# Second layer's matmuls split into 16-bit parts, attention's sequence loop written out, maxima issued ahead of exponentials

## The chip, the cores and the metric

One core of a Trainium2 chip runs the whole program. The metric is device time in microseconds (us), the median over several runs. The engines are PE (TensorE, matmuls; PEld is its weight load), DVE (VectorE), ACT (ScalarE), POOL (GpSimd) and SP (SyncE, which issues the DMAs). Each engine runs its own instructions in order and waits on semaphores for the others.

## The reference

The input x is 8 sequences of 512 tokens with 128 features, float32. Four layers follow each other, each as `x = x + layernorm(layer(layernorm(x)))`:

1. A GRU with 256 hidden units over the 512 tokens of each sequence, and a projection back to 128 features (`w_out`). The recurrence is sequential in the token.
2. A feed-forward layer with 8 experts: logits from `gate_W`, the best expert per token, `relu(x wi^T + wi_b + lora_i(x))` of width 512 with a rank-4 correction of that expert, and `wo` back to 128.
3. Attention with 16 heads of width 16, a causal mask, a position term, a smeared key, a silu gate and an output projection.
4. A SwiGLU feed-forward layer of width 384 with integer weights.

## The kernel before

The code is one program in four blocks, each with a hand-written order for every engine.

**Set-up** transposes and splits the GRU's weights into a high and a low fp16 part (W1, W2 for the state, V1, V2 for the input), and writes the normalised, transposed first 128 tokens of all sequences into Y1 and Y2 (fp16 high and low part). Their layout is `[feature, token, sequence]`, so the tokens of one sequence lie 16 bytes apart.

**GRU block.** 512 steps; a step treats all 8 sequences at once. Gate sums lie in PSUM: pR, pZ, pN. PE's `steps` does 36 products of a 128x128 fp16 weight tile with 8 columns of the state (L653): first those with the state's high part G1, then those with its low part G2, and then `inject` puts the next steps' biases (L661, a 3-row bf16 matmul) and input products (L666) into PSUM: two bias and six input matmuls in steps with k = 0 and 1, four bias ones at k = 2, six input ones at k = 3, where k is the step modulo U = 4. ACT's `steps` takes tanh of pR (tr, L805), of pZ (tz, L807) and of v_ (n_, L809). DVE's `steps` makes u_, v_, zg, zn, the new state's high part (L896), the full state HR (L901) and the low part (L903). After every four steps SP copies HR to HS, which keeps all the states.

A function `schedule` lays other work between the steps: every step is a slot, and sixteen slots make a unit. In the first 128 steps (8 rounds q of 16 slots) `prepare` normalises and transposes the remaining tokens of sequence q (ACT L849 writes Y1, DVE L1004 writes Y2, 384 tokens each) and transposes all later weights. In the remaining 384 steps each unit holds one tile of 128 tokens: `early(u, s)` does the GRU's output projection, its layer norm and the gate logits of tile u, and `late(u - 1, s)` does the expert layer of the tile before. 24 of the 32 tiles run beside steps; the last 8 units have no steps left to run beside, and then a last `late` follows. The matmuls of `early` and `late` have float32 operands: L714 and L716 (`woutT`), L725 (transpose of XF), L729 (`gaT`, gate and lora_A), L732 (transpose of the masked ML), L739 (`wiT`) and L743 (`lbT`), four each, and L750 (`woT`), four. ACT copies HB from HS (L822), XFT (L826), LAT (L831) and makes the relu with its bias in four pieces (L834). DVE does the sums, moments and normalisations (L912 to L980).

**Attention block.** `sequences` calls `body(b, ...)` for the 8 sequences: b = 0 written out, 1 to 4 in a hardware loop of two rounds with two bodies each, 5, 6 and 7 written out. A body has 4 head groups of 11 items. On PE, `item` first does `exp_item` (scores transposed, into bank pair p_e, L1460 and mask L1463, read by ACT's exp L1603) and then `maxima` for the group two ahead (scores into bank pair p_x, L1444 and mask L1447, reduced by DVE L1700). Projections, transposes and products with V lie between items. An item waits for the reader of its bank from two items before.

**The last block** is the SwiGLU layer; the change leaves it alone.

Of the kernel before, what the change touches and what calls it, by code (L numbers as in the profile page):

```python
# [17 lines left out]
BF16 = mybir.dt.bfloat16  # L18
# [20 lines left out]
U = 4  # L39
# [19 lines left out]
def build(nc, x_d, gamma_d, beta_d, w_ih_d, w_hh_d, b_ih_d, b_hh_d, w_out_d, b_out_d,  # L59
# [4 lines left out]
    with top:  # L64
# [14 lines left out]
        woutT = sb(top, "woutT", [P, HC, D])  # L79
        wiT = sb(top, "wiT", [P, F])  # L80
        woT = sb(top, "woT", [P, FC, D])
        gaT = sb(top, "gaT", [P, E + E * R])
        lbT = sb(top, "lbT", [E * R, F])
# [76 lines left out]
        Y1 = sb(gru_scope, "Y1", [P, S + U, B], FP16)  # L160
        Y2 = sb(gru_scope, "Y2", [P, S + U, B], FP16)
        HS = sb(gru_scope, "HS", [P, S, HC, B])
        brow = sb(gru_scope, "brow", [3, 8 * P], BF16)
        ones3 = sb(gru_scope, "ones3", [3, U * B], BF16)
        wguT = sb(gru_scope, "wguT", [P, 2 * HID])
# [19 lines left out]
        with ctx:  # L185
# [88 lines left out]
            def _(pool):  # L274
# [9 lines left out]
                pool.memset(Y1[:, S:, :], 0.0).then_inc(consts.sem, 1)  # L284
                pool.memset(Y2[:, S:, :], 0.0).then_inc(consts.sem, 1)
# [50 lines left out]
            def _(act):  # L336
# [22 lines left out]
                for i in range(2):  # L359
                    act.wait_ge(yT_ps.sem, i + 1)  # L360
                    act.activation(Y1[:, 0:P, 4 * i:4 * i + 4].rearrange("p s b -> p b s"),
                                   PS[:, i, :].rearrange("p (b s) -> p b s", b=4), ACT.Copy).then_inc(y_high.sem, 1)
# [4 lines left out]
            def _(dve):  # L367
# [65 lines left out]
                for i in range(2):  # L433
                    dve.wait_ge(y_high.sem, i + 1)
                    y = slice(4 * i, 4 * i + 4)
                    dve.tensor_tensor(Y2[:, 0:P, y].rearrange("p s b -> p b s"), PS[:, i, :].rearrange("p (b s) -> p b s", b=4),
                                      Y1[:, 0:P, y].rearrange("p s b -> p b s"), ALU.subtract).then_inc(y_low.sem, 1)

        SLOTS = P // B
        ctx = ExitStack()  # L440
        with ctx:
# [6 lines left out]
            G1 = sb(ctx, "G1", [P, HC, B], FP16)  # L448
            G2 = sb(ctx, "G2", [P, HC, B], FP16)
# [44 lines left out]
            HB = sb(ctx, "HB", [P, HC, P])  # L494
# [5 lines left out]
            XFT = sb(ctx, "XFT", [P, P])  # L500
# [6 lines left out]
            LAT = sb(ctx, "LAT", [E * R, P])  # L507
            INT = sb(ctx, "INT", [P, FC, P])
# [6 lines left out]
            p_gy = PS[:, 6, 0:D]  # L515
            p_xfT = PS[:, 7, 0:P]
            p_ga = PS[:, 7, 0:E + E * R]
            p_laT = PS[0:E * R, 6, 0:P]
            p_base = [PS[:, 6 if c == 2 else 7, 0:P] for c in range(FC)]
            p_dn = PS[:, 6, 0:D]  # L520

            hb = signal("hb_copied", HC)
# [17 lines left out]
            ml = signal("masked_lora_ready")  # L540
            laT_ps = signal("loraT_ps")
            laT = signal("loraT_ready")
            base = signal("base_ps", FC)
            inter = signal("inter_ready", FC)
# [53 lines left out]
            def _(sp):  # L598
                with sp.Fori(0, S // (2 * U)) as q:
                    for p in range(2):  # L600

                        sp.wait_ge(g_ready.sem, sp.snap(q * (2 * U) + U * (p + 1)))
                        at = sp.snap(q * (2 * U) + U * p)
                        sp.dma_start(HS[:, bass.ds(at, U)].rearrange("p u c b -> p u (c b)"),
                                     HR[:, p]).then_inc(hr_out[p].sem, 16)
# [4 lines left out]
            def _(pool):  # L610
# [18 lines left out]
                def late(u, s):  # L629
                    if s == 14:  # L630
# [13 lines left out]
            def _(pe):  # L644
# [4 lines left out]
                def product(gate, p, k, mc, kc, W, G):  # L649
# [3 lines left out]
                    return pe.matmul(bank[:, p, o:o + B], W[:, kc, w:w + P], G[:, kc, :],  # L653
                                     start=False, stop=True, skip_group_check=True)

                def inject(gates_at, p, rows, start):
                    for bank, first, bias, chunk in gates_at:
                        for mc in range(HC):
                            o = bank[:, p, first:first + U * NSTEP].rearrange("p (u c b) -> p u c b", u=U, c=HC)[:, :, mc, :]
# [1393 lines left out]
```

## Time and profile before

| what | us |
|---|---|
| median of 3 runs | 1976.41 (1976.2 to 1980.02) |
| time of the profiled execution | 1975.0 |
| its span, first to last instruction | 1973.1 |
| PE busy | 1683.9 (85%) |
| PEld busy | 1261.1 (64%) |
| DVE busy | 1177.6 (60%) |
| ACT busy | 739.8 (37%) |
| POOL busy | 362.9 (18%) |
| mean granted TensorE clock | 0.964 |

Busy shares are averages over stages with different limits. The rows that follow later take one stage at a time. A matmul's printed duration reaches from its issue to its end and overlaps the next one's, so its cost to the engine is read from one start to the next. A clock of 1.00 is 2.4 GHz and 0.5 is 1.2 GHz.

### The profile page before, as it was taken

What the parts mean: (1) busy time and instruction counts of PE and PEld (TensorE: products, weight loads), DVE (VectorE), ACT (ScalarE), POOL (GpSimd) and SP (SyncE); (2) the same over time, 40 slices, a digit from 0 to 9 for tenths busy, and PEclk for the clock granted to TensorE, in tenths of its full rate; (3) what the DMA queues carried; (4) which work ended last, traced back from release to release, by engine and by line L of the source; (5) the groups of instructions that cost most, each with busy time, mean ns of one, the idle gap of its engine ahead of it and who ended that gap; (6) DMA issues with size and microseconds to landing.
All of it is one profiled execution on the core that took longest, in us unless ns stands there. A gap on an engine that the chain in (4) does not pass through costs nothing. (4 is left out here: it accounts for less than half of the span.)

```text
span 1973.1 us, 68602 instructions
## 1 busy us (share of the span) xinstructions
PE 1683.9 (85%) x27122; PEld 1261.1 (64%) x27137; DVE 1177.6 (60%) x5580; ACT 739.8 (37%) x2556; POOL 362.9 (18%) x597
## 2 busy tenths in 40 slices
PE   4888878999999999999999988348988889897857
PEld 3676767888888888888888866224545455444423
DVE  5666666665655665556556544436676566675366
ACT  2333332222222222222222222014665566665645
POOL 2010100000000000000000012362123313411244
PEclk9999999999999999999999999977999899998979
DMA  5000000000000000000000000076436625732001
GB/s 121 7 8 7 7 7 7 5 3 4 3 5 5 4 4 3 4 3 4 3 4 3 4 1 0 2 118 99 60 54 91 99 25 79 101 56 28 1 6 38
DMA packets 80562, 53.56 MB, mean 27 GB/s; under 512 B 28558, under 2 KB 80166, under 8 KB 80422
## 3 DMA queue, kind: packets, MB, share of 16 engines
q1 hardware_dynamic: 78566, 51.54, 16.5%
q8 instruction: 97, 1.59, 0.3%
q14 instruction: 43, 0.35, 0.1%
q10 hardware_dynamic: 1856, 0.07, 0.1%
HBM read 31.84 MB, written 15.47 MB: 24 GB/s over the span
## 5 line engine op out<-in xcount | busy, mean ns | idle before, releaser
L653 PEld LDWEIGHTS PS<-G,W 128*128 128x128 f16 x18432 | 548.4, 105 | 181.2 <-DVE G L896 164.4
L653 PE MATMUL PS<-G,W 128*128 128x8 f16 x18432 | 577.7, 168 | 89.3 <-DVE G L896 85.5
L1700 DVE TENSOR_REDUCE MX<-PS 128x1 f32<-128x512 f32 (+3 forms) x352 | 223.0, 636 | 191.9 <-PE PS L1447 182.5
L805 ACT ACTIVATE tr<-PS 128x16 f32<-128x16 f32 x512 | 96.3, 188 | 578.3 <-PE PS L653 578.3
L1603 ACT ACTIVATE PT<-PS 128x512 f32<-128x512 f32 (+1 forms) x352 | 193.8, 559 | 171.0 <-PE PS L1463 167.1
L882 DVE SCALAR_TENSOR_TENSOR u_<-tr,PS 128x16 f32<-128x16 f32 x512 | 89.1, 174 | 274.7 <-PE PS L653 253.5
L666 PE MATMUL PS<-Y,V 128*128 (+1 forms) x2322 | 175.3, 192 | 0.0
L807 ACT ACTIVATE tz<-PS 128x16 f32<-128x16 f32 x512 | 93.7, 183 | 189.9 <-PE PS L653 189.9
L1444 PE MATMUL PS<-KS,QS 99*128 99x256 bf16 (+3 forms) x512 | 136.6, 319 | 31.6 <-DMA KS<-k_parts 20.7
L615 POOL TENSOR_TENSOR rt<-mv,eps 128x1 f32<-128x1 f32 x96 | 18.2, 189 | 746.9 <-DVE mv L917 746.9
L661 PE MATMUL PS<-ones,brow 3*128 3x32 bf16 x1032 | 141.0, 195 | 4.8 <-PEq L185 3.9
L1460 PE MATMUL PS<-QS,KS 102*128 102x256 bf16 (+3 forms) x512 | 133.3, 312 | 5.0 <-issue 2.9
L890 DVE SCALAR_TENSOR_TENSOR zg<-tz,HR 128x16 f32<-128x16 f32 x512 | 89.4, 175 | 74.9 <-ACT tz L807 74.9
L666 PEld LDWEIGHTS PS<-Y,V 128*128 128x128 f16 x2322 | 110.5, 106 | 19.1
L809 ACT ACTIVATE n_<-v_ 128x16 f32<-128x16 f32 x512 | 110.4, 216 | 21.8 <-DVE v_ L887 21.8
L1490 PE MATMUL PS<-PT,VV 128*32 128x512 f32 (+3 forms) x1024 | 101.2, 468 | 0.6 <-ACT PT L1603 0.5
L743 PE MATMUL PS<-LAT,lbT 32*128 32x128 f32 x256 | 100.9, 495 | 0.0
L903 DVE TENSOR_TENSOR G<-HR,G 128x16 f16<-128x16 f32 x512 | 89.4, 175 | 17.4
L896 DVE SCALAR_TENSOR_TENSOR G<-zg,zn 128x16 f16<-128x16 f32 x512 | 89.3, 174 | 17.6
L1460 PEld LDWEIGHTS PS<-QS,KS 102*128 102x128 bf16 x512 | 45.6, 103 | 84.4 <-issue 41.9
L739 PE MATMUL PS<-XFT,wiT 128*128 128x128 f32 x256 | 98.3, 488 | 0.8 <-ACT INT L834 0.5
L887 DVE TENSOR_TENSOR v_<-u_,PS 128x16 f32<-128x16 f32 x512 | 87.4, 171 | 17.6
(324 smaller groups left out, 2677.4 us busy)
## 6 DMA issues: line engine op xcount, KB each, us to landing
QS<-q_parts SPq DMA_DIRECT2D x48, 256.0 KB
KS<-k_parts SPq DMA_DIRECT2D x48, 256.0 KB
q_parts<-PQ SPq DMA_DIRECT2D x16, 384.0 KB, 12.8
k_parts<-PK SPq DMA_DIRECT2D x16, 384.0 KB, 13.1
HS<-HR SPq DMA_DIRECT2D x128, 32.0 KB, 1.7
X<-in_L_attn_x_dram SPq DMA_DIRECT2D x4, 512.0 KB, 8.8
out_dram<-X SPq DMA_DIRECT2D x8, 256.0 KB, 2.3
s_hh<-in_L_attn_w_hh_dram SPq DMA_DIRECT2D x1, 768.0 KB, 5.5
```

What stands on the lines that cost most here:

```text
L653: return pe.matmul(bank[:, p, o:o + B], W[:, kc, w:w + P], G[:, kc, :], start=False, stop=True, skip_group_check=True)
L661: pe.matmul(o, brow[:, (bias + mc) * P:(bias + mc + 1) * P], ones3[:, :], start=start and mc == 0, stop=False, skip_group_check=True)
L666: pe.matmul(o, V[:, w], Y[:, rows, :].rearrange("p s b -> p (s b)"), start=False, stop=False, skip_group_check=True)
L739: pe.matmul(p_base[c], wiT[:, c * P:(c + 1) * P], XFT[:, :], start=True, stop=False)
L743: pe.matmul(p_base[c], lbT[:, c * P:(c + 1) * P], LAT[:, :], start=False, stop=True).then_inc(base.sem, 1)
L805: act.activation(tr[:, :], pR[:, p, o:o + NSTEP], ACT.Tanh, scale=gate_scale).then_inc(hn_tr.sem, 1)
L809: act.activation(n_[:, :], v_[:, :], ACT.Tanh, scale=n_scale).then_inc(n_ready.sem, 1)
L1444: pe.matmul(bank[:, a * w:(a + 1) * w], QS[0:KM, p, 4 * g + i, q], KS[0:KM, p, 4 * g + i, 0:w], start=(a == 0), stop=False, skip_group_che ...
L1460: pe.matmul(bank[:, a * w:(a + 1) * w], KS[0:KF, p, 4 * g + i, j * P:(j + 1) * P], QS[0:KF, p, 4 * g + i, j * P:S], start=(a == 0), stop=F ...
L1490: last = pe.matmul(p_o[32 * i:32 * i + 32, j * P:S], VV[:, p, j, 4 * g + i, :], PT[:, j % 2, i, 0:S - j * P], start=(j == 0), stop=(j == N ...
L1603: act.activation(PT[:, j % 2, heads[0]:heads[-1] + 1, 0:w], p_e[:, k % 2, 0:len(heads) * w].rearrange("p (a w) -> p a w", w=w), ACT.Exp).t ...
L1700: dve.tensor_reduce(MX[:, g % 2, heads[0]:heads[-1] + 1, NT - 1 - it], p_x[:, k % 2, 0:len(heads) * w].rearrange("p (a w) -> p a w", w=w), ...
```

## The change

It has three parts.

1. *Second layer on 16-bit parts.* `woutT`, `gaT`, `wiT`, `woT` are scaled by a power of two and split into two fp16 parts (OU, GA, WI, DN); `lbT` into three bf16 parts stacked in LB and LB2; the bias `wi_b` into three bf16 rows (`wibr`). Activations are split likewise: HB comes as two parts out of HS, XH and XL, IH and IL, and ML as six bf16 pieces (MP). One float32 matmul becomes three fp16 ones. The relu is one piece of 512 columns. The scale is taken out again by `finv` in the DVE operations that read PSUM. The weights are split during the first 128 steps, in rounds 3 to 6 of `prepare`.
2. *Layouts in the GRU.* HS and the new GB keep the state as fp16 high and low part; SP copies GB, not HR. Y1 and Y2 become `[feature, sequence, token]`. The gate sums in PSUM have the step innermost, so a product writes its 8 columns 16 bytes apart, ACT and DVE read 16 values 16 bytes apart, and `inject` writes 32 columns in one piece but reads Y in runs of four.
3. *Attention.* The loop over sequences 1 to 4 is written out (SP keeps its own loop), and on PE `maxima` comes before `exp_item`.

```diff
-        Y1 = sb(gru_scope, "Y1", [P, S + U, B], FP16)
-        HS = sb(gru_scope, "HS", [P, S, HC, B])
+        Y1 = sb(gru_scope, "Y1", [P, B, S + U], FP16)
+        HS = sb(gru_scope, "HS", [P, S // U, 2, U, NSTEP], FP16)
...
-                    o = NSTEP * k + B * mc
-                    return pe.matmul(bank[:, p, o:o + B], W[:, kc, w:w + P], G[:, kc, :],
+                    at = mc * U * B
+                    state = GB[:, p, part, k - 1, :] if k else GB[:, 1 - p, part, U - 1, :]
+                    return pe.matmul(bank[:, p, at:at + U * B].rearrange("p (b u) -> p b u", u=U)[:, :, k], W[:, kc, w:w + P],
...
+                TERMS = ((0, 0), (0, 1), (1, 0))
                 def early(u, k, b, s):
+                    if s in (2, 3):
+                        for h, w in TERMS:
+                            last = pe.matmul(p_gy, HB[:, h, c, :], OU[w][:, c, :], ...)
...
+                    if s == 12:
+                        for h, w in TERMS:
+                            last = pe.matmul(p_ga, (XH, XL)[h][:, :], GA[w][:, :], ...)
                 def late(u, s):
+                    if s == 1:
+                        pe.wait_ge(mlp.sem, mlp.value(pe, u))
+                        pe.transpose(p_laT[:, 0:P], MP[:, 0:4, :]..., identb[:, :])
+                        pe.transpose(p_laT[0:2 * E * R, P:2 * P], MP[:, 4:6, :]..., identb[:, :])
+                    for c in {3: (0, 1), 4: (2, 3)}.get(s, ()):
+                        pe.matmul(o, wibr[:, at], ones3w[:, :], start=(c == 0), ...)
+                        for h, w in TERMS:
+                            pe.matmul(o, WI[w][:, at], (XH, XL)[h][:, :], ...)
+                        pe.matmul(o, LB[:, at], LAT[:, :], ...)
+                        last = pe.matmul(o, LB2[:, at], LAT2[:, :], ...)
+                    for c in {8: (0, 1), 9: (2, 3)}.get(s, ()):
+                        for h, w in TERMS:
+                            last = pe.matmul(p_dn, (IH, IL)[h][:, c, :], DN[w][:, c, :], ...)
...
+                        for h in range(2):
+                            act.activation(HB[:, h, :, :]..., src..., ACT.Copy).then_inc(hb.sem, 1)
+                    if s == 5:
+                        act.activation(IH[:, :, :]..., p_base, ACT.Relu).then_inc(inter.sem, 1)
...
+                    if s == 11:
+                        dve.tensor_tensor(XL[:, :], p_xfT, XH[:, :], ALU.subtract).then_inc(xl.sem, 1)
+                    if s == 15:
+                        dve.tensor_copy(MP[:, 2:5, :], ML...).then_inc(mlp.sem, 1)
+                        dve.tensor_tensor(MR_[:, :], ML[:, :], MP[:, 2, :], ALU.subtract).then_inc(mlp.sem, 1)
                 def late(u, s):
+                    if s == 0:
+                        dve.tensor_copy(MP[:, 0:2, :], MR_...).then_inc(mlp.sem, 1)
+                        dve.tensor_tensor(MP[:, 5, :], MR_[:, :], MP[:, 0, :], ALU.subtract).then_inc(mlp.sem, 1)
+                    if s in (6, 7):
+                        dve.scalar_tensor_tensor(IL[:, c, :], p_base..., 0.0, IH[:, c, :], ALU.max, ALU.subtract)
+                    if s == 10:   # was 12
+                        dve.scalar_tensor_tensor(T2[:, :], p_dn, finv[:, 4:5], wob[:, :], ALU.mult, ALU.add)
+                    if s == 11:   # was 13: stats;  s == 12 (was 14): aggregate
                     if s == 14:   # was 15
                         normal(u, 2, N2, T2[:, :], n2)
                         dve.tensor_tensor(tile(u), tile(u), N2[:, :], ALU.add)
...
+                    if q == 3 and s == 2:
+                        biggest(fmx[:, 2:3], flat3(woT))      # one of six maxima of the weights
+                    if q == 5 and s == 3:
+                        low(flat3(DN[1]), flat3(woT), fS[:, 2:3], flat3(DN[0]))   # one of the low parts
...
-                with eng.Fori(0, 2) as q:
-                    for k in range(2):
-                        c = lambda d: eng.snap(q * 2 + (k + 1 + d))
-                        body(c(0), 1 - k, c(-1), c(1), c(2))
-                body(5, 1, 4, 6, 7)
+                for b in range(1, B - 2):
+                    body(b, b % 2, b - 1, b + 1, b + 2)
...
-                    exp_item(b, p, g, j, n)
                     if ahead:
                         maxima(*ahead, j, n)
+                    exp_item(b, p, g, j, n)
```

## Rows read from the trace of the kernel before

**Rows 1.** Busy time by stretch: from:to, length, engines, PEclk, DMA share, GB/s.
```profile
36.30:299.20 262.90, 212.46 (x5509) 184.15 (x5506) 165.87 (x990) 81.26 (x409) 23.78 (x57) 1.00 0.03 7
299.20:1145.00 845.80, 805.97 (x17028) 693.28 (x17025) 511.09 (x3178) 237.48 (x1337) 62.53 (x164) 1.00 0.02 4
1145.00:1250.00 105.00, 88.83 (x306) 65.91 (x303) 40.33 (x183) 23.33 (x72) 22.80 (x60) 1.00 0.00 1
1348.60:1864.00 515.40, 451.23 (x3748) 249.89 (x3760) 326.87 (x825) 321.32 (x598) 148.34 (x152) 0.94 0.43 62
```
**Rows 2.** Timeline of ACT over one unit: start, duration, instruction, [idle before, releaser].
```profile
720.10 0.18 ACT L805 ACTIVATE tr<-PS 128x16 f32<-128x16 f32 x1 [1.07 <-PE PS L653]
...
728.93 0.18 ACT L805 ACTIVATE tr<-PS 128x16 f32<-128x16 f32 x1 [1.07 <-PE PS L653]
...
731.97 0.18 ACT L805 ACTIVATE tr<-PS 128x16 f32<-128x16 f32 x1 [2.18 <-PE PS L653]
...
755.64 0.18 ACT L805 ACTIVATE tr<-PS 128x16 f32<-128x16 f32 x1 [1.07 <-PE PS L653]
```
**Rows 3.** Timeline of PE in that unit: slot 4, then slots 11 and 12.
```profile
728.33 1.12 PE L653 MATMUL PS<-G,W 128*128 128x8 f16 x36
729.38 0.20 PE L661 MATMUL PS<-ones,brow 3*128 3x32 bf16 x1
...
729.95 0.78 PE L739 MATMUL PS<-XFT,wiT 128*128 128x128 f32 x2
730.65 0.79 PE L743 MATMUL PS<-LAT,lbT 32*128 32x128 f32 x2
...
744.64 1.12 PE L653 MATMUL PS<-G,W 128*128 128x8 f16 x36 [0.20 <-DVE G L896]
745.62 0.32 PE L666 MATMUL PS<-Y,V 128*128 x6
745.78 0.78 PE L750 MATMUL PS<-woT,INT 128*128 128x128 f32 x2
746.58 1.12 PE L653 MATMUL PS<-G,W 128*128 128x8 f16 x36
```
**Rows 4.** Timeline of PE in attention: four bf16 matmuls, then the next line.
```profile
1766.18 0.40 PE L1460 MATMUL PS<-QS,KS 102*128 102x128 bf16 x4
1766.41 0.39 PE L1463 MATMUL PS<-maskL,identb 128*128 128x128 bf16 x4
```
**Rows 5.** Timeline of DVE, slot 6 of that unit, up to the next step.
```profile
735.58 0.17 DVE L903 TENSOR_TENSOR G<-HR,G 128x16 f16<-128x16 f32 x1
...
736.06 0.29 DVE L941 TENSOR_TENSOR X<-X,N 128x128 f32 x1
736.36 0.17 DVE L882 SCALAR_TENSOR_TENSOR u_<-tr,PS 128x16 f32<-128x16 f32 x1
```
**Rows 6.** Groups by line and form, 20 to 345 us: count, busy us, mean ns, idle.
```profile
L1004 DVE TENSOR_TENSOR Y<-PS,Y 128x384 f16<-128x384 f32 x8 | 14.9, 1867 | 0.0
L849 ACT ACTIVATE Y<-PS 128x384 f16<-128x384 f32 x8 | 14.9, 1862 | 0.0
L846 ACT ACTIVATE wdT<-PS 128x384 f32<-128x384 f32 x1 | 0.5, 472 | 0.0
```
**Rows 7.** Groups by line and form, DVE, 1250 to 1900 us.
```profile
L1693 DVE SCALAR_TENSOR_TENSOR SP<-TH,PS 128x256 f32<-128x256 f32 x32 | 13.2, 411 | 1.8 <-ACT TH L1586 1.8
L1737 DVE RECIPROCAL RS_<-PS 128x16 f32<-128x16 f32 x32 | 7.9, 245 | 8.4 <-PE PS L1521 8.4
```
**Rows 8.** Timeline of DVE in two units that follow each other, without steps.
```profile
1196.32 0.29 DVE L933 TENSOR_TENSOR T<-X0b,PS 128x128 f32<-128x128 f32 x1 [0.73 <-PE PS L716]
...
1207.77 0.29 DVE L933 TENSOR_TENSOR T<-X0b,PS 128x128 f32<-128x128 f32 x1 [0.73 <-PE PS L716]
```
**Rows 9.** ACT's exp line L1603 in the stretches of sequences 3 and 5.
```profile
1547.66:1619.62 71.96, 24.27 (x44) 0.91 0.44 64
...
1688.57:1756.83 68.26, 24.32 (x44) 0.95 0.51 73
```

More of the change, by code:

```diff
@@ L515, in build @@
             p_gy = PS[:, 6, 0:D]
+            p_dn = PS[:, 6, 0:D]
+            p_ga = PS[:, 6, 0:E + E * R]
             p_xfT = PS[:, 7, 0:P]
[L517 to L522, printed above, removed]
+            p_laT = PS[:, 7, 0:P].bitcast(BF16)
+            p_base = PS[:, 7, :]
+            hb = signal("hb_copied", 2)
             x0 = signal("x0_ready")
@@ new lines, in late @@
+                        pe.matmul(o, wibr[:, at], ones3w[:, :], start=(c == 0), stop=False, skip_group_check=True)
+                        for h, w in TERMS:
+                            pe.matmul(o, WI[w][:, at], (XH, XL)[h][:, :], start=False, stop=False, skip_group_check=True)
+                        pe.matmul(o, LB[:, at], LAT[:, :], start=False, stop=False, skip_group_check=True)
+                        last = pe.matmul(o, LB2[:, at], LAT2[:, :], start=False, stop=True, skip_group_check=True)
@@ new lines, in late @@
+                        if c == FC - 1:
+                            last.then_inc(base.sem, 1)
+                    for c in {8: (0, 1), 9: (2, 3)}.get(s, ()):
+                        if c % 2 == 0:
+                            pe.wait_ge(ilow.sem, ilow.value(pe, u, c // 2 + 1))
+                        if c == 0 and not (isinstance(u, int) and u == 0):
+                            pe.wait_ge(t2.sem, t2.before(pe, u))
+                        for h, w in TERMS:
+                            last = pe.matmul(p_dn, (IH, IL)[h][:, c, :], DN[w][:, c, :], start=(c == 0 and h == 0 and w == 0),
+                                             stop=(c == FC - 1 and h == 1), skip_group_check=True)
@@ L771, in prepare @@
                         t = s - 7
+                        if t == 0 and q in (3, 4):
+                            pe.wait_ge(fsc.sem, fsc.value(pe, 0, 9 if q == 3 else 15))
                         pe.wait_ge(tail_y.sem, tail_y.value(pe, 0, (NT - 1) * q + t + 1))
@@ L777, in prepare @@
                             last.then_inc(tail_ps.sem, 1)
+                    if q == 3 and s == 5:
+                        pe.wait_ge(fsc.sem, fsc.value(pe, 0, 8))
+                        pe.transpose(PS[0:6, 6, 3 * P:], fmx[:, :], ident[:, :]).then_inc(fps.sem, 1)
+                    if q == 3 and s == 12:
+                        pe.wait_ge(tail_low.sem, tail_low.value(pe, 0, 4))
+                        pe.transpose(PS[0:1, 6, 3 * P:3 * P + 6], fcol[:, :], ident[0:6, 0:6]).then_inc(fps.sem, 1)
+                    if q == 4 and s == 2:
+                        pe.wait_ge(fsc.sem, fsc.value(pe, 0, 14))
+                        pe.matmul(PS[:, 6, 3 * P:3 * P + 4], onesr[:, :], frow[:, 0:4], start=True, stop=True).then_inc(fps.sem, 1)
+                    if q == 6 and s == 8:
+                        pe.wait_ge(hv.sem, hv.value(pe, 0, 4))
+                        pe.wait_ge(fsc.sem, fsc.value(pe, 0, 22))
+                        rows = PS[0:3, 7, 2 * P:].bitcast(BF16)
+                        for c in range(FC):
+                            last = pe.transpose(rows[:, c * P:(c + 1) * P], wibp[:, c, :], identb[:, :])
+                        last.then_inc(fps.sem, 1)
                     if q == 6 and s == 6:
@@ L830, in late @@
                         act.wait_ge(laT_ps.sem, laT_ps.value(act, u))
-                        act.activation(LAT[:, :], p_laT, ACT.Copy).then_inc(laT.sem, 1)
-                    for c in {2: (0,), 5: (1,), 7: (2,), 9: (3,)}.get(s, ()):
-                        act.wait_ge(base.sem, base.value(act, u, c + 1))
-                        act.activation(INT[:, c, :], p_base[c], ACT.Relu, bias=wib[:, c:c + 1]).then_inc(inter.sem, 1)
+                        act.activation(LAT[:, :], p_laT[:, 0:P], ACT.Copy).then_inc(laT.sem, 1)
@@ L836, in prepare @@
+                        act.activation(LAT2[:, :], p_laT[0:2 * E * R, P:2 * P], ACT.Copy).then_inc(laT.sem, 1)
+                    if s == 5:
+                        act.wait_ge(base.sem, base.value(act, u))
+                        if not (isinstance(u, int) and u == 0):
+                            act.wait_ge(dn.sem, dn.before(act, u))
+                        act.activation(IH[:, :, :].rearrange("p c n -> p (c n)"), p_base, ACT.Relu).then_inc(inter.sem, 1)
                 def prepare(q, s):
```

330 lines of the change are left out of this document (240 added, 90 removed).

## The prediction

> **What bounds the kernel now.** I read the stretches first. The GRU's first 128 steps take 262.9 us with PE busy 212, the other 384 take 845.8 with PE busy 806, the eight units without steps 105 with PE busy 89, attention's bodies 515 with PE busy 451 [rows 1]. So from step 128 on PE is the candidate. The timeline of one unit says how: its 16 steps take 755.64 - 720.10 = 35.54 us [rows 2], while the step from slot 11 to slot 12 takes 746.58 - 744.64 = 1.94 [rows 3]. 1.94 is the latency of the chain product, tanh, u, v, tanh, zn, state; nothing else makes that slot longer. 16 x 1.94 = 31.04, so a unit carries 4.50 us of excess. Slot 4 alone has 731.97 - 728.93 = 3.04, 1.10 of it excess [rows 2]. There PE starts the products at 728.33, `inject` at 729.38, a float32 matmul at 729.95 and another at 730.65, which together end with the next step at 731.37 (728.33 + 3.04) [rows 3]: 1.62 us of own work and then 1.42 for two float32 matmuls, 0.7 each. What a slot can take free of charge is 1.94 - 1.62 = 0.32 us at k = 0 or 1, and 1.94 - 1.14 = 0.80 at k = 3 (745.78 - 744.64) [rows 3].
>
> DVE has such a limit too. From the start of G2 (735.58) to the next u (736.36) lie 0.78 us, and slot 6 fills them to the brim: its last extra operation runs from 736.06 to 736.35 [rows 5]. What is added behind it delays u, and with it every later step.
>
> The profiled execution took 1975.0 us around a span of 1973.1, 1.4 below the median of 1976.41. The sum is made against 1975.0, and the 1.4 is added at the end.
>
> **Phase 2, PE (23 units that have steps, `early` and `late`).** Out go fourteen float32 operations of up to 0.7 us. In come 45 of 16-bit operands. A 128-column one costs (1766.41 - 1766.18) / 4 = 0.057 us from start to start [rows 4]. Changing between a 3-row operand and a 128-row one costs more: slot 4's two bias and six input matmuls take 729.95 - 729.38 = 0.57, while six input ones alone take 0.16 [rows 3], so about (0.57 - 8 x 0.027) / 3 = 0.12 per change. A base chunk of the new code is bias, three fp16, LB, LB2: 6 x 0.057 = 0.34, plus two changes of rows at least (0.57 in all), plus two more if fp16 to bf16 or 128 to 64 rows costs the same (0.81). I take 0.68, the middle, since the rows show no such pair.
> - Slot 3 (k = 3): 1.14 + 3 x 0.057 for the projection + 2 x 0.68 = 2.67, excess 0.73 (0.5 to 1.0).
> - Slot 4 (k = 0): 1.62 + 1.36 = 2.98, excess 1.04 (0.8 to 1.3).
> - Slots 8 and 9: 1.62 + 6 x 0.057 = 1.96, and perhaps one change more: 0.1 for both.
> - Slots 1, 2, 10, 12: two transposes, three products, one float32 transpose, three 40-column products. They fit in the free time, as the longer ones of before did in slots 2 and 10.
>
> PE's excess is 1.9 us per unit (1.3 to 2.5).
>
> **Phase 2, DVE.** The low part IL adds two operations of 256 columns out of PSUM, 0.41 each by L1693 [rows 7]. Slot 6 is full [rows 5], so the first delays u by 0.4; slot 7 has only moments (0.29) and takes the second with 0.05. The second normalisation moves from slot 15 to slot 14, behind the cast and ML: two operations more in a slot that held three small ones, 0.4 over. Slot 15 and the loop's end get MP and MR_, slot 0 two more MP operations behind X0; each is near 0.2 with its wait, and together they pass the 0.78 by 0.45. DVE's excess is 1.3 (0.8 to 1.6). These are other slots than PE's, so both add: 3.2 against 4.50 before. Gain 1.3 per unit, 23 x 1.3 = **30 us** (9 to 55). ACT has over 1.0 us idle before each tr [rows 2] and takes HB, LAT2 and the 512-column relu in it; without that cover each would cost its 0.25 to 0.6.
>
> **Phase 1.** 262.9 - 128 x 1.94 = 14.6 us of excess in eight rounds [rows 1]. The operations behind it are L849 and L1004, 1.86 and 1.87 us for 384 fp16 values written 16 bytes apart; the same 384 columns written in one piece take 0.47 [rows 6]. With Y contiguous both fall below 0.7 and fit their gaps. That gives back some 12. The Trainium skill says the same of the direction ("SBUF — State Buffer", Door 1: accesses that hit a 16-byte line fewer than twice pay for it); the trace agrees, by 4.9 ns a value against 1.2. Against it stand the weights' maxima and parts in rounds 3 to 6: about ten DVE operations of 256 or 512 columns, five of them behind other work in slots 0 to 3 or 8 and 0.3 over each, and a dozen small ones that fit. Cost 2 to 4. Net gain **9** (6 to 12). Set-up makes two such strided writes of 512 columns on each of ACT and DVE, at 4.9 ns a value 2.5 us each; the bias rows' chain ends late as well, so of the 3 to 4 us saved on DVE I count **2** (0 to 3).
>
> **The step itself.** The products now write 8 columns 16 bytes apart, and tr, u_ and v_ read 16 values 16 bytes apart. No row has that. A product is issued every 0.03 us (36 in 1.05 [rows 3]) and has room. For the reads the nearest row is the reciprocal L1737, 16 values 128 bytes apart out of PSUM, 0.245 against 0.17 of u_ [rows 5, 7]; but a reciprocal is another operation. Lower end: the input products have the same count with a contiguous target, 0. Upper end: 3 x 0.075 = 0.22 us a step, 512 x 0.22 = 115. I take 0.01 a step, **5 us** lost, since the operations' time is mostly fixed.
>
> The Trainium skill speaks against this part ("SBUF — State Buffer", Door 1): in PSUM, lines are 8 bytes, and any access that isn't contiguous slows matmuls a lot. By that rule the products would lose their room and the sum would come out above 1975; it is the first rival.
>
> **The eight units without steps.** From one T to the next is 1207.77 - 1196.32 = 11.45 us [rows 8]. PE is 85% busy there [rows 1], but less PE work does not shorten it by as much: with float32 gone, the chain T, moments, POOL, N1, moments, POOL, XF, logits, ML, MP, X0 is left. It loses about 0.9 (ML's wait behind the old T2, queueing behind float32) and gains XL (0.35), MP (0.4), and the first IL of 0.4 plus the wait for a relu that comes only after all four base chunks (4 x 0.68 = 2.7 after T), ahead of the second moments: 0.7 to 1.5. Per unit +0.7 (-0.4 to +1.9), in eight **6 us** lost (-3 to +15).
>
> **Attention.** The loop's second round costs: the body in it takes 71.96 against 68.26 for the written-out body 5 [rows 9], and the one before it ends with the same kind of stall. Written out, that is 3.7 + 2.5, **6 us** gained (3 to 8). The code grows by two bodies; the written-out ones show no stall for it. Maxima first: PE's order of the pair changes relative to the work between items only. Where exp would wait for ACT, a 0.5 us maximum now runs in the wait; where the maximum waits for DVE, exp now stands behind it. I cost it at 0 (-5 to +5).
>
> **Sum.** 1975.0 - 30 - 9 - 2 + 5 + 6 - 6 = 1939; with 1.4 for the median **1940**.
>
> **Rivals.**
> 1. *The strided PSUM side slows each step* (the slower side). Place: product, tanh and u, v of all 512 steps. Price: x per step, 512x; the gains without the step's term are 41, so from 0.08 us a step the kernel is no faster. At 0.15 it is 1976 - 41 + 77 = 2012. For it: the 0.245 of L1737 and the slow strided writes of Y. Against it: the one is another operation, the others are two-byte writes to SBUF and not four-byte reads of PSUM. Chance 0.10.
> 2. *Base chunks are cheap and DVE's spill is small*: 16-bit switches cost nothing, excess 2.1 instead of 3.2. Another 25 us: 1915. For it: in rows 4 a 102-row and a 128-row operand follow each other with no gap. Chance 0.22.
> 3. *The excess only changes engines*: slots 3 and 4 at their upper end, DVE 1.6 and the unhidden units +1.9. Phase 2 then gains 9, the units lose 15: 1940 + 21 + 9 = 1970. For it: slot 6 is full already. Chance 0.18.
>
> My forecast, 1925 to 1955, has 0.50. The range takes in the cases 2 and 3: 1903 to 1972. What this measurement can tell from no change is 0.2%, 4 us. Below 1972.5 lie the forecast, case 2 and most of case 3: faster 0.86; same 0.04; slower 0.10, case 1.
>
> **What would show it.** In the profile after: slots 3, 4, 6, 14, 15 and 0 longer than 1.94, slots 5, 8, 9 and 12 at or near it, a unit of 34.2 us. L849's and L1004's successors below 0.7 us, and the 128 first steps in some 254 us. The floor step at 1.94 to 1.96; if it is 2.0 or more, rival 1 holds. T to T near 12 in the units without steps. Bodies 2 and 3 at 68 to 69 us. I am wrong in mechanism if slot 3 or 4 is at the floor, or if the gain comes from attention.

## The result: slower by 0.5%, and where the time went

The kernel after takes 1984.61 us (median of 8 runs, 1981.45 to 1986.91) against 1975.63 of the kernel before in the same session (8 runs). The ratio is 1.005, its 95% interval 1.0035 to 1.0065: slower. I had forecast 1940, with 1903 to 1972 as the range and 0.10 on slower, and that 0.10 rested on another mechanism. In experiments 1 and 12 one run each (2180 and 1989 us) came out slow at a lower granted clock; the medians given there include it, the ratios do not.

The profiled execution took 1986.3 us. Its page, engines and granted clock:

```profile
span 1984.4 us, 69118 instructions
...
PE 1591.1 (80%) x27657; PEld 1163.9 (59%) x27657; DVE 1228.8 (62%) x5833; ACT 739.6 (37%) x2505; POOL 363.4 (18%) x597
...
PEclk6555555555555555555555555565999999998978
```

PE's busy time fell by 92.8 us (from 1683.9) while the time rose: the work that went was not where the time was, or its removal came with something worse. The three rows below are the first 128 steps, the other 384, and the units without steps, with the columns of [rows 1].

```profile
33.89:286.37 252.48, 214.48 (x5514) 185.18 (x5512) 163.54 (x1018) 78.36 (x421) 24.22 (x57) 0.50 0.03 7
286.37:1151.03 864.66, 741.39 (x17401) 622.89 (x17399) 547.48 (x3341) 244.72 (x1291) 63.27 (x166) 0.50 0.02 4
1151.03:1254.62 103.59, 53.71 (x370) 32.97 (x368) 49.51 (x211) 19.22 (x49) 19.11 (x50) 0.50 0.00 0
```

From these and the same marks in the trace of before (first and last tanh `tr`, last T, first and last body of attention):

| stretch | before | after | difference | by the prediction |
|---|---|---|---|---|
| set-up, to the first `tr` | 36.3 | 33.9 | -2.4 | -2 |
| steps 0 to 127 | 262.9 | 252.5 | -10.4 | -9 and +1 of the floor |
| steps 128 to 511 | 845.8 | 864.7 | **+18.9** | -30 and +4 of the floor |
| last `tr` to last T (eight units without steps) | 85.7 | 103.6 | **+17.9** | +6 |
| last T to attention's first exp | 117.9 | 121.2 | +3.3 | 0 |
| attention's bodies 0 to 6 | 473.0 | 456.3 | -16.7 | -6 |
| the rest | 151.5 | 152.3 | +0.8 | 0 |

T is the sum of the GRU's projection and X0b, which DVE makes once in every unit. "The floor" is the 1.94 us of a step whose slot nothing else makes longer, and a slot's excess is what it takes above that. Two lines are wrong by much, 45 and 12 us, and a third, attention, is 11 better than forecast. The first two have the second layer in common.

**The slots.** Slots 3 and 4 of a unit on ACT: from one `tr` to the next is the slot's length, as in [rows 2].

```profile
759.53 0.18 ACT L870 ACTIVATE tr<-PS 128x16 f32<-128x16 f32 x1 [0.76 <-PE PS L683]
763.03 0.18 ACT L870 ACTIVATE tr<-PS 128x16 f32<-128x16 f32 x1 [2.64 <-PE PS L683]
766.70 0.18 ACT L870 ACTIVATE tr<-PS 128x16 f32<-128x16 f32 x1 [2.80 <-PE PS L683]
768.64 0.18 ACT L870 ACTIVATE tr<-PS 128x16 f32<-128x16 f32 x1 [0.59 <-PE PS L683]
```

Slot 3 takes 3.50, slot 4 3.67, slot 5 1.94; I had forecast 2.67, 2.98 and the floor. PE's timeline of slot 3 shows what the two base chunks cost (start, duration, instruction; the cost of one is read from its start to the next start):

```profile
760.48 0.28 PE L779 MATMUL PS<-ones3w,wibr 3*128 3x128 bf16 x1
760.70 0.39 PE L781 MATMUL PS<-XH,WI 128*128 128x128 f16 x2
760.88 0.31 PE L781 MATMUL PS<-XL,WI 128*128 128x128 f16 x1
760.99 0.31 PE L782 MATMUL PS<-LAT,LB 128*128 128x128 bf16 x1
761.24 0.28 PE L783 MATMUL PS<-LAT,LB 64*128 64x128 bf16 x1
761.45 0.28 PE L779 MATMUL PS<-ones3w,wibr 3*128 3x128 bf16 x1
```

One chunk is 761.45 - 760.48 = 0.97 us, not 0.68. From XL to LB, two 128-row matmuls that follow each other, it is 0.11 (0.107 from the unrounded starts); in attention it was 0.057 [rows 4]. Bias row to XH takes 0.22, LB to LB2 0.25, LB2 to the next bias 0.21, more than 0.107 each time the count of rows changes (3 to 128, 128 to 64, 64 to 3); fp16 to bf16 (XL to LB) costs nothing. The whole chunk takes 0.97 - 6 x 0.107 = 0.33 for three such changes, 0.11 each.

**Why 0.107.** The granted clock. The page of before shows 9s over the GRU and [rows 1] a 1.00, the page of after 5s, for the same stage. It isn't that the change lowered it: the trace of before holds no clock record ahead of 1282.1 us from the span's start, and where there is none the view prints 1.00. That of after has one from 13.3 us on (0.5, for 1297 us). The kernel before itself reads both ways: of its eight runs beside experiment 1, five have a mean clock of 0.96 to 0.97 and three one of 0.64, at 1971 to 1978 and 1970 to 1979 us. Two later kernels, whose GRUs are alike to the instruction, show it within one stage; here are 840 us of their steps, first e2_layout, then e5_parts:

```profile
290.00:1130.00 840.00, 800.82 (x16849) 687.05 (x16848) 505.71 (x3141) 235.04 (x1322) 62.09 (x163) 1.00 0.02 4
```
```profile
290.00:1130.00 840.00, 801.02 (x16849) 687.32 (x16848) 505.31 (x3141) 235.13 (x1322) 62.42 (x163) 0.50 0.02 4
```

Same instructions, PE busy to 0.03%, and one reads 1.00 and the other 0.50. So the pace must be read from the matmuls. Where the view has records, 0.107 for a 128-column one goes with 0.5, which is 1.2 GHz, and 0.056 with 1.0 (experiment 4 has both). Attention, from which I took 0.057, runs at 2.4 most of the time. The Trainium skill ("TensorE: Matmul & The Clock Gate", section "Wait — 56ns, not 53.3ns?") gives 106.7 ns from start to start for 128 columns at the low level and 55.6 at the high one; this case's traces agree with both. The 36 matmuls of 8 columns take 1.07 us at the low level and 0.99 at the high one (1136.33 - 1135.26 and 1185.84 - 1184.85 in experiment 4's trace), 0.03 each at both, which is why [rows 3] did not show the clock to me, who looked at those alone.

### The profile page after: what moved, and what is told of

It reads as the page before. It is cut to its first block and busy times, and to the rows that moved or that the text cites. A ratio compares the mean times of both kernels' runs of the same rounds, so it can differ in the third digit from the quotient of the medians.

```text
span 1984.4 us, 69118 instructions
## 1 busy us (share of the span) xinstructions
PE 1591.1 (80%) x27657; PEld 1163.9 (59%) x27657; DVE 1228.8 (62%) x5833; ACT 739.6 (37%) x2505; POOL 363.4 (18%) x597
## 5 line engine op out<-in xcount | busy, mean ns | idle before, releaser
L683 PE MATMUL PS<-GB,W 128*128 128x8 f16 x18432 | 580.1, 175 | 161.3 <-DVE GB L1002 156.2
L683 PEld LDWEIGHTS PS<-GB,W 128*128 128x128 f16 x18432 | 538.7, 105 | 226.9 <-DVE GB L1002 219.8
L1646 PEld LDWEIGHTS PS<-KS,QS 99*128 99x128 bf16 x512 | 45.3, 103 | 121.5 <-DVE MX L1902 61.3
L1002 DVE SCALAR_TENSOR_TENSOR GB<-zg,zn 128x16 f16<-128x16 f32 x512 | 89.5, 175 | 21.7
L994 DVE SCALAR_TENSOR_TENSOR zn<-tz,n_ 128x16 f32<-128x16 f32 x512 | 89.9, 176 | 17.7 <-ACT n_ L874 16.6
L1005 DVE TENSOR_TENSOR GB<-HR,GB 128x16 f16<-128x16 f32 x512 | 89.7, 175 | 17.4
L1649 PE MATMUL PS<-maskU,identb 128*128 128x128 bf16 x512 | 90.4, 228 | 0.0
```

The lines of the kernel that those rows point to most:

```text
L683: return pe.matmul(bank[:, p, at:at + U * B].rearrange("p (b u) -> p b u", u=U)[:, :, k], W[:, kc, w:w + P], state[:, kc * B:(kc + 1) * B] ...
L1646: pe.matmul(bank[:, a * w:(a + 1) * w], QS[0:KM, p, 4 * g + i, q], KS[0:KM, p, 4 * g + i, 0:w], start=(a == 0), stop=False, skip_group_che ...
L1649: last = pe.matmul(bank[:, (a + 1) * w - P:(a + 1) * w], identb[:, :], maskU[:, :], start=False, stop=True, skip_group_check=True)
```

## Experiments

**1. Fewer base matmuls.** The low parts of the base product are left out, on the kernel after.

```diff
-                        for h, w in TERMS:
+                        for h, w in TERMS[:1]:
                             pe.matmul(o, WI[w][:, at], (XH, XL)[h][:, :], start=False, stop=False, skip_group_check=True)
```

> The kernel after, with the base product's two low-part matmuls left out (the input's low part and the weight's low part): 8 of 24 base matmuls fewer in each unit, in slots 3 and 4, so that part of the product is less precise. Theory 1, TensorE runs at 1.2 GHz in the GRU and slots 3 and 4 end on it: a 128-column 16-bit matmul costs 0.107 us there, 8 x 0.107 = 0.86 a unit in 23 units, up to as much in the eight units without steps: 20 to 27 us below the kernel after, 1958 to 1965, and slots 3 and 4 shorter by about 0.43 each. Rival, the matmuls cost the 0.057 of attention and the loss is the vector engine's: 8 x 0.057 x 23 = 10 us at most, 1974 or more, slots 3 and 4 shorter by 0.23 each or not at all.

Measured: 1958.44 us (5 runs), ratio to before 0.9915 (0.9891 to 0.9939), 26 below the kernel after. Slots 3 and 4 on ACT:

```profile
713.44 0.18 ACT L870 ACTIVATE tr<-PS 128x16 f32<-128x16 f32 x1 [0.76 <-PE PS L683]
716.51 0.18 ACT L870 ACTIVATE tr<-PS 128x16 f32<-128x16 f32 x1 [2.21 <-PE PS L683]
719.74 0.18 ACT L870 ACTIVATE tr<-PS 128x16 f32<-128x16 f32 x1 [2.37 <-PE PS L683]
```

3.07 and 3.23: each 0.43 shorter, 4 x 0.107. In the units without steps the time from one T to the next ("T to T") fell from 13.91 to 13.06, by 8 x 0.107. That is theory 1; by attention's price each slot would be 0.23 shorter.

**2. The layout alone**, on the kernel before: Y as `[P, B, S + U]`, gate sums with the step innermost.

```diff
-                    o = NSTEP * k + B * mc
-                    return pe.matmul(bank[:, p, o:o + B], W[:, kc, w:w + P], G[:, kc, :],
+                    at = mc * U * B
+                    return pe.matmul(bank[:, p, at:at + U * B].rearrange("p (b u) -> p b u", u=U)[:, :, k], W[:, kc, w:w + P], G[:, kc, :],
```

> The kernel before, with one part of the change alone: the input sums' operand lies sequence by sequence, the gate sums step innermost; the second layer stays float32, attention as before. If the gain of the first 128 steps (262.9 to 252.5 in the two traces, -10.4) and of the set-up (-2.4) is this layout's, and the step's floor costs 0.01 x 512 = 5 us: -12 to -13 in the first steps without the weights' maxima, -2 in the set-up, +5: about 1966 (1963 to 1969). Rival, the strided sums cost 0.05 a step or more and the two-part state buffer hid it: 1985 or more.

Measured: 1960.63, ratio 0.9928 (0.9903 to 0.9953), 14 below before and lower than the 1963 to 1969 expected. The profiled execution is the slowest of its four, 1964.24; in it the first 128 steps take 251.2 (-11.7) and the set-up 33.9 (-2.4), as expected, and steps 128 to 511 only 2.3 more than before. The 384-column writes of Y, to be held against [rows 6]:

```profile
L1003 DVE TENSOR_TENSOR Y<-PS,Y 128x384 f16<-128x384 f32 x8 | 4.4, 551 | 0.0
L849 ACT ACTIVATE Y<-PS 128x384 f16<-128x384 f32 x8 | 3.8, 472 | 0.0
```

1.87 and 1.86 became 0.55 and 0.47. The strided sums cost 0.01 a step: the shortest slots went from 1.94 to 1.95.

**3 and 9. Attention.** Both edits on the kernel before, then the order of the items alone.

```diff
-                with eng.Fori(0, 2) as q:
-                    for k in range(2):
-                        c = lambda d: eng.snap(q * 2 + (k + 1 + d))
-                        body(c(0), 1 - k, c(-1), c(1), c(2))
-                body(5, 1, 4, 6, 7)
+                for b in range(1, B - 2):
+                    body(b, b % 2, b - 1, b + 1, b + 2)
...
-                    exp_item(b, p, g, j, n)
                     if ahead:
                         maxima(*ahead, j, n)
+                    exp_item(b, p, g, j, n)
```

> The kernel before, with attention's two edits alone: the loop over sequences written out, and each item's maximum ahead of the exponentials. The two traces differ by 16.7 us over attention's bodies, where I had predicted 6. If those 16.7 are the edits' own: 1959 (1957 to 1962), bodies 0 to 6 in 456 us. Rival, part of them comes from the second layer's change before it (buffers that come free earlier, the state of the queues): 1965 to 1970, bodies in 463 to 467.

> The kernel before, with the order of attention's items alone: each item's maximum ahead of the exponentials, the loop over sequences still a loop. Both edits together gave 17.8 us. By my prediction the written-out loop gives 6 and the order nothing: 1974 to 1976. By the two traces, in which even the bodies that were written out before changed (body 5 went from 68.26 to 67.7, body 0 from 61.99 to 59.1), the order carries a part: if it is the 12 that are left over, 1963 to 1965.

Measured: both 1956.85, ratio 0.9908 (0.9881 to 0.9935); the order alone 1962.99, 0.9939 (0.9916 to 0.9963). Bodies 0 to 6, from the first exp of one to the first of body 7, in before, with the order alone and with both (columns as in [rows 1]):

```profile
1348.62:1821.60 472.98, 412.42 (x3379) 229.67 (x3392) 304.79 (x759) 287.77 (x535) 139.11 (x143) 0.94 0.47 67
```
```profile
1349.30:1806.04 456.74, 403.09 (x3396) 226.64 (x3398) 310.94 (x759) 289.09 (x535) 138.79 (x144) 0.96 0.48 69
```
```profile
1349.57:1803.28 453.71, 399.44 (x3383) 225.42 (x3398) 309.12 (x759) 289.05 (x536) 139.33 (x144) 0.97 0.49 70
```

In these traces the order carries 16.2 us, the written-out loop 3.0. I had 0 and 6. The order's part is sure: e2_layout's trace, with neither edit, has 473.3 for the same stretch. The loop's is not: the eleven traces with both edits lie between 453.7 and 456.3, and only one, 456.7, has the order alone, so by them the loop is worth 0.4 to 3.0. By the medians of the whole time the order gives 11.5 and both 17.8, which leaves 6 for the loop, with intervals of about 5 us either way. The body that runs in the loop's second round, 71.96 [rows 9], takes 67.15 with the order alone, still in the loop.

**4, 7 and 8. Can the clock be raised?** Matmuls of 128 x 448 columns whose sums nothing reads are added at the end of each step's PE work: three and one on the kernel after, two on e5_parts.

```diff
                     inject((r_in, z_in, n_in, xn_in)[k], 1 - p, rows, k < 3)
+                    for _ in range(3):
+                        pe.matmul(pR[:, 1 - p, U * NSTEP:], W1[:, 0, 0:P], V1[:, 0:512 - U * NSTEP], start=False, stop=True, skip_group_check=True)
```

> The kernel after, with three matmuls of 128 x 448 16-bit columns added at the end of every step's products, into columns of a bank that nothing reads. Question: is the 1.2 GHz of the GRU tied to how narrow its matmuls are? Theory 1a, yes: the granted clock rises to 1.0 somewhere in the GRU, an added matmul takes 0.19 us, a base matmul 0.057, and slots 3 and 4 are longer than their neighbours by 1 us together and not by 3.3. Theory 1b, the clock stays at 0.5 whatever the columns: an added matmul takes 0.37, each step is longer by 0.8 to 1.1 us, the kernel by 400 to 560, and slots 3 and 4 stand 3.3 above their neighbours as before.

> The kernel after, with one matmul of 128 x 448 16-bit columns at the end of each step's products, where three made the granted clock rise and fall (0.779 over the span) and cost 240 us, part of it by two waits of 2.7 and 3.9 us at the end of each pass of the loop. If one is enough to hold the clock at 1.0: slots 3 and 4 near 2.5 and 2.7, steps at 1.92, 1940 or less. If it is not: 0.37 more in the steps with no time left, 5 to 8 slots a unit at up to 0.37, 2010 to 2040, clock near 0.64 over the span. With 32 more instructions a unit in place of 96 I expect the waits at the loop's end to be gone.

> The kernel of the parts without the second layer's change (layout and attention's edits), with two matmuls of 128 x 448 16-bit columns at the end of each step's products. If the granted clock is 1.0 for most of the GRU: a float32 128-column matmul falls from 0.43 to 0.22 us a pair of passes, a unit from 35.5 to 33 or less, 23 x 2.5 = 58 us below its parent: 1890. If it toggles as with three: steps at 2.0 to 2.7 in half the units, 1950 to 2050. If it stays at 0.5: 0.3 to 0.5 more in each of 512 steps, 2100 to 2200.

Measured: with three 2221.03 us (2 runs; the profiled one 2235.0, clock 0.779 over the span), with one 2039.93 (2 runs), with two on e5_parts 2126.12. None pays: the ratios are 1.125, 1.034 and 1.077. But with three the clock went up and down, and that gives the same instructions at both levels in one trace. A base chunk of slot 3, where the granted clock was 1.0:

```profile
1183.56 0.22 PE L781 MATMUL PS<-ones3w,wibr 3*128 3x128 bf16 x1
1183.71 0.28 PE L783 MATMUL PS<-XH,WI 128*128 128x128 f16 x2
1183.84 0.22 PE L783 MATMUL PS<-XL,WI 128*128 128x128 f16 x1
1183.89 0.22 PE L784 MATMUL PS<-LAT,LB 128*128 128x128 bf16 x1
1184.04 0.23 PE L785 MATMUL PS<-LAT,LB 64*128 64x128 bf16 x1
1184.20 0.23 PE L781 MATMUL PS<-ones3w,wibr 3*128 3x128 bf16 x1
```

0.64 us. The same chunk of the same kernel an earlier unit, at 0.5:

```profile
1133.32 0.28 PE L781 MATMUL PS<-ones3w,wibr 3*128 3x128 bf16 x1
...
1134.29 0.28 PE L781 MATMUL PS<-ones3w,wibr 3*128 3x128 bf16 x1
```

0.97. The prediction's 0.68 would have been nearly right at a clock that this stage doesn't have. One matmul of 448 columns a step left the clock at 0.5 over all steps, and the time is as expected for that case; two on e5_parts raised it to a mean of 0.57 between 290 and 1300 us. The three also brought a wait of another kind: at the end of most passes of the later loop over units PE stands two times, 3.91 and 2.75 us in one of them, for "issue", and the queue for instruction code moves 16 KB pieces there (17 in 80 us, where the kernel after has none). Between 690 and 1380 us such waits are 91.6 us in sum. A unit then has 776 matmuls; with the 728 of the kernel after, and the 744 of the one with one added, the wait is absent. But the earlier loop of the same kernel has 776 a pass too, and no such wait, so the count alone is not the cause; what else it takes is not shown.

**5. The parts without the second layer's:** layout and attention's two edits.

> The kernel before with three parts of the change together, the layout and attention's two edits, and without the second layer on 16-bit parts. The layout alone gave 14 us, attention alone 17.8. If they add and the second layer's parts are the whole loss: 1975.6 - 14 - 17.8 = 1944 (1940 to 1949), 40 below the kernel after. If the parts share a gain (attention's start depends on how the tail before it ends): 1950 to 1960.

Measured: 1946.5, ratio 0.9865 (0.9841 to 0.9888): 27 us, where layout and attention gave 14 and 17.8 alone. The parts add to within 5 us. So the second layer on 16-bit parts, as it is ordered in the change, costs 1984.6 - 1946.5 = 38 us; it is the whole loss, and takes the other parts' gain with it.

**6. The same matmuls in another order:** both chunks' biases, then the 128-row ones, then the 64-row ones.

```diff
+                        for c in cs:
+                            pe.matmul(p_base[:, at[c]], wibr[:, at[c]], ones3w[:, :], start=(c == 0), stop=False, skip_group_check=True)
+                        for c in cs:
                             for h, w in TERMS:
...
+                        for c in cs:
+                            last = pe.matmul(p_base[:, at[c]], LB2[:, at[c]], LAT2[:, :], start=False, stop=True, skip_group_check=True)
```

> The kernel after, with the base product's matmuls of slots 3 and 4 in another order and none fewer: both chunks' bias rows, then their eight 128-row matmuls, then the two 64-row ones. A slot then changes the count of rows 3 times instead of 6 or 7. If a change costs its own 0.11 to 0.14 us: 0.36 a slot, 0.72 a unit, in 23 units 17 us, with up to 6 in the units without steps: 1962 to 1968, slots 3 and 4 at 3.14 and 3.30. If only the number of matmuls counts: 1984, slots as in the kernel after.

Measured: 1962.82, ratio 0.9945 (0.9928 to 0.9961), 22 below the kernel after with not one instruction fewer; T to T 13.24.

```profile
715.32 0.18 ACT L874 ACTIVATE tr<-PS 128x16 f32<-128x16 f32 x1 [0.76 <-PE PS L683]
718.49 0.18 ACT L874 ACTIVATE tr<-PS 128x16 f32<-128x16 f32 x1 [2.30 <-PE PS L683]
721.82 0.18 ACT L874 ACTIVATE tr<-PS 128x16 f32<-128x16 f32 x1 [2.46 <-PE PS L683]
```

3.17 and 3.33: 0.33 less each, for three changes of rows fewer in each slot. So the count of changes costs time by itself, beside the count of matmuls.

**10 and 11. Other slots.** One chunk in each of slots 3 to 6, and what follows later by one to two slots; then also by kind of operand: four bias rows in slot 3, six input matmuls in slots 4 and 5 each, LB and LB2 in slot 6. The diff is that of the second.

```diff
-                    for c in {3: (0, 1), 4: (2, 3)}.get(s, ()):
+                    if s == 3:
+                        for c in range(FC):
+                            pe.matmul(o(c), wat(wibr, c), ones3w[:, :], start=(c == 0), stop=False, skip_group_check=True)
+                    for c in {4: (0, 1), 5: (2, 3)}.get(s, ()):
+                        for h, w in TERMS:
+                            pe.matmul(o(c), wat(WI[w], c), (XH, XL)[h][:, :], start=False, stop=False, skip_group_check=True)
+                    if s == 6:
+                        for c in range(FC):
+                            pe.matmul(o(c), wat(LB, c), LAT[:, :], start=False, stop=False, skip_group_check=True)
+                        for c in range(FC):
+                            last = pe.matmul(o(c), wat(LB2, c), LAT2[:, :], start=False, stop=True, skip_group_check=True)
```

> The kernel after, with the same instructions in other slots: one base chunk in each of slots 3 to 6 in place of two in slots 3 and 4, and everything that follows it later (relu 7, low parts 8 and 9, down product 9 and 10, T2 11, moments 12 and 13). If each slot may take its free time once (0.48 at slot 3, 0.32 at the others): excess 0.49 + 3 x 0.65 = 2.44 instead of 3.26, 19 us in 23 units. In the units without steps the second moments no longer stand behind the low part: T to T 11.9 instead of 13.9, 14 to 16 us. Sum: 1950 (1945 to 1957). If the wait of the units without steps is on TensorE and not on this order, T to T stays at 13.9: 1965.

> The kernel after, with the base product ordered by kind of operand over four slots: four bias rows in slot 3, six input matmuls in slots 4 and 5 each, the LoRA product (four 128-row, then four 64-row matmuls) in slot 6; the rest as in the one with a chunk a slot. By the prices of the low clock (0.107 a matmul, 0.12 a change of rows) and the free time of each slot: excess 0.2 + 0.32 + 0.32 + 0.78 = 1.6 instead of 3.26, 38 us in 23 units, and 14 to 16 in the units without steps: 1932 (1928 to 1942), below the kernel of the parts without the second layer (1946). If a hidden cost of the changed slots takes it back (the low parts in slots 8 and 9, where the vector engine has the second normalisation): 1945 to 1955.

Measured: one chunk a slot 1954.45, ratio 0.989 (0.9867 to 0.9914), slots 3 to 6 at 2.53, 2.69, 2.69, 2.14. Staged: **1924.26, ratio 0.9739 (0.9716 to 0.9762)**, 60 below the kernel after. Its slots 3 to 6 on ACT:

```profile
731.40 0.18 ACT L875 ACTIVATE tr<-PS 128x16 f32<-128x16 f32 x1 [0.76 <-PE PS L683]
733.49 0.18 ACT L875 ACTIVATE tr<-PS 128x16 f32<-128x16 f32 x1 [1.22 <-PE PS L683]
735.73 0.18 ACT L875 ACTIVATE tr<-PS 128x16 f32<-128x16 f32 x1 [1.38 <-PE PS L683]
737.97 0.18 ACT L875 ACTIVATE tr<-PS 128x16 f32<-128x16 f32 x1 [1.37 <-PE PS L683]
740.32 0.18 ACT L875 ACTIVATE tr<-PS 128x16 f32<-128x16 f32 x1 [1.49 <-PE PS L683]
```

2.09, 2.24, 2.24, 2.35: above 1.95 each they have 1.12 together, where the kernel after has 3.26 in slots 3 and 4. The first is within its 1945 to 1957; the second is below its 1928 to 1942. In both, the share of the steps came out larger than forecast (27 us for 19, 53 for 38), and that of the units without steps smaller (1.7 and 5.4 us for 14 to 16): T to T is 13.67 with one chunk a slot and 13.14 staged, not 11.9. The low part ahead of the second moments was not what held these units. My account of them was wrong.

**12. The units without steps.** What holds them? In the staged kernel, at the end of such a unit:

```profile
1152.93 0.25 DVE L1081 CAST MP<-ML 128x96 bf16<-128x96 f32 x1
...
1154.20 0.45 POOL L652 TENSOR_TENSOR X0b<-X,bout 128x128 f32<-128x128 f32 x1 [2.00 <-DVE X L1034]
1154.25 0.44 DVE L1090 TENSOR_TENSOR MP<-MR_,MP 128x32 bf16<-128x32 f32 x1
1154.83 0.28 PE L772 MATMUL PS<-identb,MP 128*128 128x128 bf16 x1 [4.78 <-DVE MP L1090]
...
1155.29 0.82 PE L748 MATMUL PS<-OU,HB 128*128 128x128 f16 x6
...
1156.22 0.35 DVE L1040 SCALAR_TENSOR_TENSOR T<-PS,finv,X0b 128x128 f32<-128x128 f32 x1 [1.52 <-PE PS L748]
```

X0b is there at 1154.65. T waits for L748, which stands on PE behind the transposes of MP, and these idled PE for 4.78 us until DVE's fourth MP operation.

The first two MP operations move from slot 15 to 14, the other two from slot 0 of `late` to slot 15 of `early`:

```diff
-                    if s == 15:
+                    if s == 14:
...
                         dve.tensor_tensor(MR_[:, :], ML[:, :], MP[:, 2, :], ALU.subtract).then_inc(mlp.sem, 1)
-
-                def late(u, s):
-                    if s == 0:
+                    if s == 15:
                         dve.wait_ge(mlp.sem, mlp.value(dve, u, 2))
```

> The staged kernel with the router's three 16-bit parts MP formed earlier in the vector engine's order: the first two operations in slot 14 ahead of the third normalisation, the other two in slot 15 ahead of X0. Question: why do the units without steps still take 13.14 us from T to T, where before they took 11.45, although the base product is now shorter than in the kernel after? Theory: there the projection's matmuls stand behind the two transposes of MP, and these wait for MP, whose last operation stands behind the third normalisation and X0 and ends 0.6 us before T's matmuls begin. Then T to T falls to 11.6 to 12.0, 9 to 12 us in eight units; in the 23 units with steps the same operations sit a slot earlier, -0.1 to +0.2 each, 0 to +4. Sum: 1924.3 - 11 + 2 = 1915 (1911 to 1921). Rival: the last of T's operands is X0b, behind the normalisation, X0 and GpSimd, which the change doesn't shorten: T to T at 13, 1922 to 1928.

Measured: 1922.1 (6 runs), ratio 0.9748 (0.9734 to 0.9762): not told apart from the staged kernel, and above the 1911 to 1921 expected. What held the units without steps is shown all the same:

```profile
1147.37 0.35 DVE L1040 SCALAR_TENSOR_TENSOR T<-PS,finv,X0b 128x128 f32<-128x128 f32 x1 [0.81 <-PE PS L748]
...
1159.14 0.35 DVE L1040 SCALAR_TENSOR_TENSOR T<-PS,finv,X0b 128x128 f32<-128x128 f32 x1 [0.81 <-PE PS L748]
```

T to T is 11.77, and last `tr` to last T 89.2 instead of 98.2. Of the 2.46 by which T to T was longer in the kernel after than in that before, the base product's order took back 0.77 (13.91 to 13.14) and MP's place 1.37; 0.32 are left. But the steps gave it back. In slot 14 DVE now has MP, MR_, the normalisation and its sum, and the u of the next slot waits for them; this slot is, on ACT:

```profile
727.07 0.18 ACT L875 ACTIVATE tr<-PS 128x16 f32<-128x16 f32 x1 [1.08 <-PE PS L683]
729.99 0.18 ACT L875 ACTIVATE tr<-PS 128x16 f32<-128x16 f32 x1 [1.09 <-PE PS L683]
```

2.92 instead of 2.30; slots 0 and 1 get 0.37 back, a unit is 0.30 longer, and steps 128 to 511 take 819.2 instead of 811.5.

## Why the prediction was wrong, by its own steps

- *The price of a 16-bit matmul, 0.057 from [rows 4]: this is the step that failed.* It was read in attention, at the high clock, and applied in the GRU, which runs at the low one. Base chunk 0.68 (measured 0.97), so slot 3's excess 0.73 (1.55), slot 4's 1.04 (1.72), slots 8 and 9 0.1 together (0.29 each). PE's excess per unit is 3.8 us instead of 1.9. 23 x 1.9 = 44 of the 45 us that phase 2 was off. Experiments 1, 4 and 6 show price and place.
- *The bounds.* "1.3 to 2.5" did not hold 3.8, since both ends used the same 0.057. The other price in that sum, 0.12 for a change of rows, was read in the GRU and is right (0.11). Of "0.57 or 0.81 per chunk", two changes or four, the truth is in the middle, as assumed: three changes, none of them fp16 to bf16.
- *DVE's excess of 1.3 a unit*: measured 1.02, in slot 7 (0.23), 15 (0.35) and 1 (0.44). What I put on slots 6 and 14 shows in slots 7 and 15, whose u it delays. Slot 0 is 0.37 over too, but that isn't the work of MP: with MP gone from it (experiment 12) 0.33 stay. The rows point to the turn of the hardware loop: slot 0 takes 2.32 in the later loop, 2.62 where the outer loop turns too, and 1.95 in the first 128 steps, which have no loop; before the change u stood 0.43 for "issue" there. I had counted all of the 4.50 as going, this part too. DVE's share was forecast high by about as much, so the two errors cancel, by luck.
- *4.50 of excess before, 31.04 of floor*: right as a reading; the sum per unit after is 36.37 against the forecast 34.2.
- *Phase 1* -9 (and +1): right, -10.4. *Set-up* -2: -2.4. *Strided sums* +0.01 a step: right, 1.94 to 1.95; rival 1 is out. The rule of the Trainium skill that I weighed there ("SBUF — State Buffer", Door 1) is not borne out for products of 8 columns in PSUM in this kernel.
- *Eight units without steps* +6: +17.9. I had the chain through base product and low part; experiments 10 and 12 show that it is PE's order, with the projection behind transposes that wait for the last MP (1.37 of the 2.46 us a unit), and with the base product's price and order (0.77). "MP 0.4" was costed as work on DVE, and not as something that PE's queue stands behind.
- *Attention* -6: -16.7 in the kernel after, -19.3 in experiment 3. The order was put at 0 and gives 16.2: this is a second term that was mis-sized. The loop's share was put at 6; the traces have at most 3.0 and the medians do not decide. "Where exp would wait for ACT, a maximum now runs in the wait" was the right picture, and its size was never worked out. Which wait it fills was not traced further.
- *Rivals.* Rival 3, the excess only changes engines, comes nearest in kind: the excess stayed and grew, but on PE itself. No rival had the clock. The 3.3 us between last T and first exp stay unexplained; that stretch takes 117.9 to 121.3 in these kernels, without a pattern that I could tie to an edit.

## What to carry to other kernels

Take an instruction's price from the same stage, and check the clock of that stage by the pace of its matmuls, not by the clock view alone. When matmuls of different row counts are mixed, order them by row count, and spread them until each slot's free time is used once: here that turned +0.5% into -2.6% with the same matmuls, most of it in the slots beside steps. And before costing an added operation, ask who stands behind its consumer in that engine's queue.

## What the runs showed of the hardware

- PE can be 86% busy by the profile (741.39 of 864.66 us) at a granted clock of 0.5 throughout; before it first rises, in the kernel of experiment 4, PE had three more matmuls of 448 columns a step; with one more it stayed at 0.5.
- A change of row count between neighbouring matmuls costs 0.11 us at the low clock (0.97 for six with three changes) and 0.10 at the high one (0.64 - 6 x 0.056 = 0.30 for three), a change between fp16 and bf16 nothing (0.107 from XL to LB).
- Products that write 8 float32 values 16 bytes apart in PSUM, with reads of 16 such values, cost 0.01 us a step; 384 2-byte values written 16 bytes apart in SBUF cost 1.87 us on DVE and 1.86 on ACT, against 0.55 and 0.47 in one piece.
- In experiment 4 PE stands at the later loop's end for 2.7 and 3.9 us, with code being loaded. Its pass has 776 matmuls; with 744 (experiment 7) there is no such wait, and none in the earlier loop with 776.
